# A fused decoder layer with a gated recurrence: the setup by pairs of chunks, in one block with the loop

## The reference

```python
x  = layernorm(x)                                   # z; also the residual of the block
h  = rms(x) * w_norm_in
h  = silu(conv_b + sum(pad(h)[:, j:j+T] * conv_w[:, j] for j in range(4)))     # causal, 4 taps
q, k, v = h @ wq, h @ wk, h @ wv;  q, k = q / (norm(q) + eps), k / (norm(k) + eps)   # per head
sd = h @ w_spike;  ab = silu(h @ w_au + b_au) @ w_ad + b_ad;  bb = h @ w_beta + b_beta
# for each of 512 steps t:
mem = 0.9 * mem + sd[t];  spike = mem > 0.5;  mem = mem - 0.5 * spike
alpha = sigmoid(ab[t] + alpha_spike * spike)        # 1 where no unit of the head has fired
beta  = sigmoid(bb[t] + sum(spike * beta_spike))    # 0 where no unit of the head has fired
s = alpha * s;  s = s - beta * k (k s);  s = s + beta * k v;   out[t] = q s
```

## Time and profile before

| | |
|---|---|
| median of 3 runs | 1237.21 us (1233.9 to 1239.5) |
| profiled execution | 1248.79 us, span 1247.1 us |
| TensorE busy, share of the span | 87% |
| VectorE busy | 59% |
| ScalarE busy | 40% |
| GpSimd busy | 16% |
| mean granted TensorE clock | 0.93 of full |

### The profile page before, as it was taken

How to read it: one execution, slowest core, us unless ns; L and a number is a source line. 1 busy time by engine, 2 the same in 40 slices (tenths; PEclk the granted TensorE clock), 3 DMA queues, 4 the chain that set the end, 5 groups by cost and what they waited for, 6 DMA issues and landing times. The chain is left out here.

```text
span 1247.1 us, 40866 instructions
## 1 busy us (share of the span) xinstructions
PE 1078.8 (87%) x17220; PEld 773.9 (62%) x17220; DVE 733.6 (59%) x2539; ACT 499.3 (40%) x1429; POOL 202.3 (16%) x381
## 2 busy tenths in 40 slices
PE   1587546999999999999999999699999899899987
PEld 1222124888888888888888887346556545644652
DVE  4656688668888888888877763127135333512710
ACT  1465201134444444444454444244235325525421
POOL 4100021112211222122221221202101101200210
PEclk9989655589999999999999998899899899999999
DMA  2000000000000000000000000300000000000000
GB/s 84 0 1 0 1 0 1 2 4 3 4 4 4 3 4 4 4 3 4 4 4 26 5 4 3 117 8 1 1 9 1 10 1 9 9 1 1 1 9 8
DMA packets 11219, 11.35 MB, mean 9 GB/s; under 512 B 1515, under 2 KB 9311, under 8 KB 11039
## 3 DMA queue, kind: packets, MB, share of 16 engines
q1 hardware_dynamic: 11039, 8.75, 2.3%
HBM read 7.70 MB, written 1.05 MB: 7 GB/s over the span
## 5 line engine op out<-in xcount | busy, mean ns | idle before, releaser
L1027 ACT COPY work<-banks 128x128 f32<-128x128 f32 x160 | 43.0, 269 | 168.3 <-PE banks L881 168.3
L851 PE MATMUL banks<-work 64*64 64x64 f32 x3072 | 103.6, 234 | 5.3 <-DVE gates L725 4.4
L881 PE MATMUL banks<-work,gates 64*64 64x32 f32 x2560 | 105.8, 221 | 2.5 <-issue 2.5
L901 PE MATMUL banks<-work 64*64 64x32 f32 x2560 | 105.9, 223 | 0.4 <-ACT work L1027 0.4
L302 DVE SCALAR_TENSOR_TENSOR mom<-gates 128x16 f32<-128x16 f32 x512 | 101.4, 198 | 5.7
L298 DVE SCALAR_TENSOR_TENSOR gates<-mom,gates 128x16 f32<-128x16 f32 x512 | 96.6, 189 | 11.4 <-ACT gates L414 6.7
L881 PEld LDWEIGHTS banks<-work,gates 64*64 64x64 f32 x2560 | 93.7, 139 | 15.3 <-issue 12.8
L725 DVE COPY_PREDICATED gates<-work,banks 128x256 f32<-128x256 uint32 x192 | 101.8, 530 | 1.1
L730 DVE TENSOR_TENSOR work<-work,banks 128x128 f32<-128x128 f32 x128 | 36.8, 288 | 104.5 <-PE banks L891 103.1
L891 PEld LDWEIGHTS banks<-work 64*64 64x64 f32 x2048 | 74.7, 140 | 33.1 <-issue 22.6
L901 PEld LDWEIGHTS banks<-work 64*64 64x64 f32 x2560 | 92.6, 140 | 0.5 <-ACT work L1027 0.5
(11 more groups left out here) (228 smaller groups left out, 2360.6 us busy)
## 6 DMA issues: line engine op xcount, KB each, us to landing
work<-in_x_dram SPq DMA_DIRECT2D x4, 256.0 KB, 2.9
out_dram<-work SPq DMA_DIRECT2D x4, 256.0 KB, 2.3
gates<-in_w_ff_dram SPq DMA_DIRECT2D x3, 256.0 KB, 3.6
wv_sb<-in_wv_dram SPq DMA_DIRECT2D x1, 512.0 KB, 4.5
work<-in_w_out_dram SPq DMA_DIRECT2D x1, 512.0 KB, 4.2
gates<-in_x_Wq_dram SPq DMA_DIRECT2D x1, 512.0 KB, 5.2
gates<-in_x_Wk_dram SPq DMA_DIRECT2D x1, 512.0 KB, 5.1
gates<-in_x_Wv_dram SPq DMA_DIRECT2D x1, 512.0 KB, 6.0
```

What stands on the lines that cost most here:

```text
L851: last = pe.matmul(level_out(l)[to, a], KS[rows, n.two, hp], late[rows, hp], start=True, stop=True)
L881: last = pe.matmul(packed(psZX, l)[rows, hp], EA[rows, n.three, l, hp], first_half(X, l)[rows, hp], start=True, stop=True)
L901: last = pe.matmul(packed(psXT, l)[rows, hp], Z[rows, l - 1, hp], second_half(XT[:, n.two], l)[rows, hp], start=True, stop=True)
L1027: ac.copy(first_half(Z[:, l - 1], l), packed(psZX, l)).then_inc(z_ok, 1)
```

## The change

The three blocks become one. Work is cut into four pairs of chunks (`NPAIR = 4`, 512 columns each, all sequences) in place of sequences. Part by part:

- x comes in four transfers ahead of the weights. Row sums are VectorE's, squares with their sums ScalarE's (`square_rows`), all further factors GpSimd's on 4 or 12 columns (`scales`), and the two norms are applied by ScalarE with scale and bias (`normal`, `centred`), the second only after the last of the first chunk's scan inputs.
- The convolution is four accumulating matmuls with diagonal weights made by ScalarE (`taps`, `convolve`). Nine matmuls on `ident` stand at the head of TensorE's queue.
- The scan starts behind pair 0. Its steps 0 to 63 stand among the `keep_h` and `keep_au` of pairs 0 to 3; projections of pair 0 (`project(0, 2)` to `project(6, 2)`) run beside it.
- Gates 0 to 3 stand behind step 63, and beside them on TensorE and ScalarE the projections of pairs 1 to 3. Steps 64 to 127 stand among and behind the gates. The loop starts at body -3.
- The norms of q and k are inverted twice, once for pair 0 and once for pairs 1 to 3 together, in place of four times. The scalings of pair 0 stand among the gates, those of pairs 1 to 3 (24 instructions, 6 spreads) in bodies -3 and -2 (`ramp`).
- Buffers of the rounds take the places of setup buffers, and waits are added for that.

The core of the diff (waits, buffers, constants and GpSimd's masks left out):

```diff
-                ve.wait_ge(tr_out, NT // 4)
-                ve.wait_ge(w_loaded, 16 * 10)
-                for b in range(B):
-                    ve.tensor_scalar(conv[:, b], h0T[:, b, 0:T], v("conv_w", 0), v("conv_b"), ALU.mult, ALU.add)\
-                        .then_inc(conv_ok, 1)
-                for j in range(1, PAD + 1):
-                    for b in range(B):
-                        ve.wait_ge(conv_ok, B * (j - 1) + b + 1)
-                        ve.scalar_tensor_tensor(conv[:, b], h0T[:, b, j:j + T], v("conv_w", j), conv[:, b],
-                                                ALU.mult, ALU.add).then_inc(conv_ok, 1)
...
-            for i in range(-7, ROUNDS + 1):
+            for i in range(-3, ROUNDS + 1):
                 body(*[at_round(i + k) for k in (-1, 0, 1, 2, 3)], at_gate(i + 7), at_gate(i + 6),
-                     at_scan(i + 11))
+                     at_scan(i + 11), i + 3 if i < -1 else None)
...
+                scales(0, 1, 0)                      # GpSimd: nine small instructions, two of them powers
+                keep_late(LEVELS - 1)
+                gp.wait_ge(masks, 2 + 3 * LEVELS)
+                gp.memset(wad_sb[R:P], 0.0).then_inc(padded, 1)
+                gp.wait_ge(padded, 1)
+                gp.memset(auT_all[R:P], 0.0).then_inc(padded, 1)
+                gp.wait_ge(padded, 2)
+                scales(1, NPAIR - 1, 7)
...
+                keep_h(0)                            # VectorE
+                done = scan_to(10, 0)
+                keep_au(0)
+                done = scan_to(14, done)
+                keep_h(1)
...
+                keep_au(3)
+                done = scan_to(C - done, done)
+
+                spikes(first[0])
+                invert(0)
+                drive(first[0])
+                spikes(first[1])
+                done = scan_to(2, done)
+                alpha(first[0])
+                for j in range(3):
+                    scale(0, j)
+                done = scan_to(1, done)
+                beta(first[0])
...
+                drive(first[3])
+                done = scan_to(2, done)
+                alpha(first[3])
+                done = scan_to(2 * C - done, done)
+                invert(1)
                 rounds(body)
...
+                def convolve(k):
...
+                    for j in range(PAD + 1):
+                        last = pe.matmul(bank[k % 2][:, :], conv_diag[:, j, :], h0T[:, :, k * PAIR + j:k * PAIR + j + PAIR],
+                                         start=j == 0, stop=j == PAD)
+                    last.then_inc(conv_mm, 1)
...
+                for _ in range(9):                   # TensorE
+                    pe.matmul(bank[0][:, :], ident[:, :], ident[:, :].unsqueeze(1).broadcast_to([P, B, P]), start=True, stop=True)
+                turn_in(0)
+                pe.wait_ge(w_loaded, 16 * 10)
+                convolve(0)
+                for n in range(HP):
+                    drive_in(n)
+                gate_in(0)
+                project(0, 2)
...
+                for k in range(NPAIR):
+                    turn_z(k)
+                project(8, 4)
+                spike_sums(first[0])
+                spread_norm(0, 0)
+                project(12, 1)
+                beta_sums(first[0])
+                project(13, 2)
+                spike_sums(first[1])
...
+                for n in range(HP + 2, NSD):
+                    drive_in(n)
                 rounds(body)
...
+                square_rows(2)                       # ScalarE
+                taps()
+                normal(0)
+                square_rows(3)
+                keep_h0(0)
+                stairs()
+                soft_conv(0)
+                for n in range(HP):
+                    keep_drive(n)
+                normal(1)
...
+                soft_au(3)
+                norm_root(0)
+                centred(0)
...
+                keep_z(3)
+                keep_qk(8, 4)
+                soft_alpha(first[0])
...
+                soft_alpha(first[3])
+                keep_qk(23, 9)
+                norm_root(1)
+                for n in range(HP, NSD):
+                    keep_drive(n)
                 rounds(body)
...
+                        if ramp == 0 and l != 3:     # in VectorE's body; TensorE's has spread_norm there
+                            four_scales(1 + l // 4, (l % 4) // 2 if l < 4 else l - 4)
+                        if ramp == 1 and l < 3:
+                            four_scales(3, l - 1)
```

More of the change, by code:

```diff
@@ L612, in _ @@
             def _(gp):
-                for t in (state, EA, Z):
-                    gp.memset(t, 0.0).then_inc(zeroed, 1)
-                gp.wait_ge(zeroed, 3)
+                gp.memset(ident[:, :], 0.0).then_inc(consts, 1)
+                gp.wait_ge(consts, 1)
+                gp.affine_select(out=ident[:, :], in_=ident[:, :], compare_op=ALU.not_equal, fill=1.0,
+                                 base=0, pattern=[[-1, P]], channel_multiplier=1).then_inc(eye_ok, 1)
+                gp.memset(half[:, :], -0.5).then_inc(consts, 1)
@@ L616, in _ @@
+                gp.wait_ge(cleared, 1)
                 gp.wait_ge(folded, NFOLD)
@@ new lines, in scan_to, with invert @@
+                def scan_to(steps, done):
+                    for t in range(done, done + steps):
+                        charge(ve, t)
+                        fire(ve, t)
+                    return done + steps
+                def invert(n):
+                    ve.wait_ge(nrm_ok, n + 1)
+                    if n:
+                        ve.wait_ge(bc_mm, 2)
+                    ve.tensor_scalar(nrm_e, nrm, 1e-6, None, ALU.add).then_inc(nrm_add, 1)
+                    ve.wait_ge(nrm_add, n + 1)
+                    ve.reciprocal(nrm_e, nrm_e).then_inc(nrm_inv, 1)
@@ new lines, in _ @@
+                ve.wait_ge(folded, NFOLD)
+                first = [Gate(g) for g in range(HP)]
+                keep_h(0)
[3 more added lines that the diff above has]
+                keep_h(1)
+                done = scan_to(8, done)
+                keep_au(1)
+                done = scan_to(8, done)
+                keep_h(2)
+                done = scan_to(8, done)
+                keep_au(2)
+                done = scan_to(4, done)
@@ new lines, in _ @@
+                done = scan_to(2, done)
+                drive(first[1])
+                spikes(first[2])
+                done = scan_to(2, done)
+                alpha(first[1])
+                for j in range(4, 7):
+                    scale(0, j)
+                done = scan_to(1, done)
+                beta(first[1])
+                scale(0, 7)
+                done = scan_to(2, done)
+                drive(first[2])
+                spikes(first[3])
+                done = scan_to(2, done)
```

751 lines of the change are left out of this document (437 added, 314 removed).

## The result

Beside each other the kernel before takes 1237.2 us in the median (1233.9 to 1239.5) and the changed one 1190.53 us (4 runs, 1188.0 to 1203.9): 46.7 us less. The ratio is 0.965, with a 95% interval of 0.956 to 0.974. Some runs of each kernel are slower than its fastest by more than 1.5%, one of the kernel before here (1255.48 us) and five more in what follows, and all medians and ratios leave them out.

What follows compares the result with a forecast made beforehand. The setup was taken to be bound by turns between engines, not work; savings of 26.7 and 62.9 us less 29.6 and 18.5 given back make 41.5 us, so 1237.2 becomes 1196 us, range 1176 to 1216.

Steps and rivals of the forecast that it cites:

- part A: Setup up to the scan's first step: starts at 30.5 us (28 to 35) instead of 57.2, saving 26.7 us.
- part B: Scan steps 0 to 63 with seven insertions and 2 us of waits: 35.6 us instead of 98.5, saving 62.9 us.
- part C: Gates 0 to 3 and steps 64 to 127 beside projections: 64.4 us (48 to 78), 29.6 more than before.
- part D: Bodies -3 and -2 with 24 added scalings on VectorE: 18.5 us more (15 to 29) than 26.2 us before.
- Rival 4: Scan, steps 0 to 63: each of seven insertions waits 4.4 us for its chain; 1226 us, chance 0.06.
- rival 1: Gates 0 to 3: TensorE idles in pieces from 60 to 80 us, clock halves, gates take 12 us; 1208 us, chance 0.17.
- the 3.6 us for slow stretches: Gates and steps 64 to 127: 3.6 us added for slow clock, so body -3 begins at 130.5 us.
- Sum: End of body -2: 175.2 us instead of 216.7, 41.5 us less.
- Rounds at the same pace as before: Rounds behind body -2: untouched by the change, expected to keep their old pace.
- rival 2: Early rounds behind body -2: run at full clock, recovering 14.8 us; 1181 us, chance 0.12.
- The table loads: ScalarE between step 63 and gate 0's sigmoid: two switches of 1.28 us; the skill's drain would add some 3 us.

Runs made afterwards that it cites:

- gate 0 early: Changed kernel with gate 0's `spike_sums` behind the second `turn_z`, ahead of all projections, and `soft_alpha` ahead of `centred(3)`: median 1190.5 us, ratio 0.957.
- late drives: Changed kernel with the eight drives of pairs 2 and 3 moved from TensorE's prologue into bodies -3 and -2: median 1190.4 us, ratio 0.961.
- scalings first: Changed kernel with the 24 scalings of pairs 1 to 3 and their six spreads in one piece ahead of body -3: median 1205.0 us, ratio 0.970.
- TensorE kept busy in the kernel before: Kernel before plus 30 unused matmuls of 512 columns on `ident` in bodies -7 to -2: median 1234.3 us, ratio 0.995.
- convolution 0 on VectorE: Changed kernel with pair 0's convolution back on VectorE and four matmuls on `ident` in its place on TensorE: median 1195.9 us, ratio 0.960.
- the version that has both, with two more edits: Changed kernel with early gate 0, drives moved into bodies -3 and -2, pair 0's convolution on VectorE, seven filler matmuls on `ident`: median 1174.3 us, ratio 0.948.

## Why the prediction was right, step by step

Predicted were 1196 us (1176 to 1216) and faster with 0.95; measured are 1190.5 us. The four parts came out near their forecasts, and three of them within 2 us; that the sum hit within 6 us is in part luck. Body -2 ended 8.9 us before the forecast and the rounds behind it took 10.1 us less, while 11.6 us, by which the profile of the kernel before stood above its median, did not carry over (the profiled execution was forecast at 1207.3 us and took 1190.8).

What saved the time is read from the marks: part A 57.2 - 28.9 = 28.3 us and part B 98.6 - 34.9 = 63.7 us saved, part C 57.4 - 34.8 = 22.6 us and part D 18.9 us given back, 50.5 us in all. The runs test the overlap in part C, part D and pieces of part A. Part B, the largest, was undone in no run.

- **Part A** (forecast 30.5, measured 28.9 us). The weights landed at 12.3 us, not at 14.0, and that is the whole difference. The added transfers of x did cost 1.2 us of SyncE's queue (2.08 us for four, 0.86 before for one), but `vec` behind them took 0.50 instead of 2.05 us, so the last two loads were issued at 7.02 us, not later than before (7.42). The path behind them is the forecast's: `taps` and `normal` 2.9 us (3.1), the transposes with convolution and drive 0.66 + 5.37 + 3.70 = 9.7 us (10.5), four evacuations. The nine matmuls on `ident` were rightly costed at nothing much; the experiment without them confirms it.
- **Part B** (35.6 us, measured 63.75 - 28.86 = 34.9 us). Two microseconds of waits were taken; one wait of 2.04 us was found. Rival 4, a wait of 4.4 us at each insertion, is out.
- **Part C** (64.4 us, measured 121.17 - 63.75 = 57.4 us). This is the term that was mis-sized most. `drive` of gate 0 came at 76.2 us (forecast 77), so the 7 us of waiting behind the projections were found as 8.4. But gates follow each other every (97.47 - 76.16) / 3 = 7.1 us, not 8.6: the clock was full from 76 us to 98 us, so rival 1 is out, and projections fit into the gaps. The first half of rival 1 did happen: the granted clock was 0.74 from 60 to 80 us. It fell into the wait for gate 0, and the 3.6 us for slow stretches were not needed beside it. VectorE does 41 steps behind gate 3 in any case, so 3 x 1.5 + 3.6 = 8.1 us, less 1.4 us of longer waiting, account for the 7.0 us that this part came out short, within half a microsecond. The wait that does stand at its end is not in the sum of part C at all: the ten drives ahead of the first spread (3.72 us), shown by gate 0 early and by late drives. The forecast had these drives ending near 131 us beside VectorE's work and did not see that the spread is queued behind them.
- **Part D** (+18.5 us, measured 45.1 - 26.2 = +18.9 us). The sum is right, its parts are shifted: four scalings in a row take 2.48 us, so 24 take 14.9 and not 16.4, and the uncovered first spread costs 3.7 and not 2.1. That the other waits are hidden by the scan between the groups is shown by scalings first: without that cover five of them cost 11.1 us.
- **Sum.** Body -2 ends at 166.3, not 175.2 us: 1.6 + 0.7 + 7.0 less and 0.4 more. That gives 50.5 us less than before, not 41.5.
- **The rounds behind.** "Rounds at the same pace as before" was wrong in the profile: three rounds took 56.5 us, 10.1 us less, which is rival 2 by two thirds (14.8 us). It came through the clock, at 1.00 from 200 us on. By the seventh `keys` the two profiles are 60.3 us apart, but in the medians the gain is 46.7 us. The same was seen with TensorE kept busy in the kernel before: 17 us of the profiled span, 6 us of the median. The forecast added its marks to a profiled execution 11.6 us above the median and carried that offset over; the changed kernel's profiled execution stood at its median. The sum by the true marks (1237.2 - 50.5 = 1186.7 us) is 3.8 us below what was measured; with the three rounds and the one behind them it is 1176.9 us, 13.6 us below. Part of such a gap is scatter behind the early rounds: the rest takes 936 to 951 us in the table for the same code, 944 and 951 us in the changed kernel's own two profiles. Between unprofiled runs time goes with the clock in the main: the fastest of the 17 of the kernel before took 1231.0 us at a mean granted clock of 0.941, the slowest 1247.2 us at 0.924. In which part the unprofiled runs of the kernel before are shorter than its profile is not known, as no trace of them exists.
- **The table loads.** ScalarE's timeline of the changed kernel:

```profile
59.78 1.28 ACT L1207 ACT_TABLE_LOAD   x1
61.07 0.60 ACT L1207 ACTIVATE work<-banks 128x512 f32<-128x512 f32 x1
...
76.40 1.28 ACT L1267 ACT_TABLE_LOAD   x1
77.69 0.51 ACT L1267 ACTIVATE work<-gates,vec 128x256 f32<-128x256 f32 x1
```

Both switches cost 1.28 us, and the next activation began 0.01 us after each. The Trainium skill ("ScalarE: Activation LUTs", What ACT_TABLE_LOAD costs) adds a drain of 1.38 us to each; the trace disagrees at these two places, and the 3 us that the rule would have added did not come.

**What stays open** is why the clock recovers at different times in the early rounds. In the changed kernel it is 0.83 from 180 to 200 us, with gate 0 early and with late drives it is still about 0.5 there, though these kernels give TensorE nearly the same work. It is no chance of one execution: the changed kernel's three rounds took 56.5 us in both its profiles. No experiment separated the cause.

## What to carry to other kernels

Where no engine is full, look for what each wait stands in line for and give it something independent in between: here 64 steps of a scan and four gates went beside projections (22 us at the mark, 8 us in the median). A piece of filling hides the waits of other engines and never the busy engine's own instructions, so price it at their whole duration. When an edit moves one wait and nothing is gained, look at the queue of the other engine that the next stage needs: gate 0 early and late drives gained nothing alone, and the version that has both, with two more edits, is 17 us faster by the medians. Profile a kernel twice before a difference of two spans is put down to an edit: here the same kernel's spans differed by 6.1 us, and all of it lay where nothing had been changed.

## What the hardware showed that was not expected

- TensorE's granted clock stayed near half although the engine was almost never idle: with convolution 0 on VectorE, in the window from 180 to 200 us,

```profile
180.00:200.00 20.00, 19.03 (x317) 15.97 (x314) 12.99 (x58) 3.12 (x8) 2.64 (x7) 0.51 0.01 2
```

TensorE was busy for 19.03 of 20 us, mostly with matmuls of 64 rows and 32 or 64 columns, at a granted clock of 0.51; from 200 to 220 us, with the same lines of the kernel, it was 0.98. The Trainium skill ("TensorE: Matmul & The Clock Gate", What's actually happening) lets sustained activity lift the half rate; that held for matmuls of 512 columns (from 0.83, 0.69 and 0.54 to 1.00, 0.91 and 0.95 with 17 of them added), and in this window it did not.
- Fillers helped where they stood among the work, and not across a pause: 10.96 us of matmuls that ended 2.7 us before the next one moved no mark, and behind that pause the granted clock was 0.64 from 17 to 20 us.
- The granted clock also dips late in the kernel, by an amount that differs between executions: 0.89 from 680 to 760 us in one profile of the changed kernel, 0.73 in the other.
- The first `spikes` beside the memset of GpSimd took 4.33 us in the kernel before. With the memset moved ahead of the scan (23.91 us) it takes 0.29 us. `keep_h(0)`, which now runs beside the memset for its last 0.45 us, takes 0.75 us, as long as the later insertions do (0.74).
